# Attention normalization three slots later, its sum and the router's moments two, and a later, tighter S5 step sequence, in a hybrid layer kernel on one core

## What is computed

```python
x = x + s6(_layernorm(x), Wi, bi, Wx, bx, Wdt, bdt, A_log, Dp, Wo, bo, gamma, beta)   # "attention a"
x = x + moe(_layernorm(x), Wg, W1, W2, W3)
x = x + s5(_layernorm(x), Lambda_re, Lambda_im, B, C, D, log_step)                    # "attention b"
x = x + moe(_layernorm(x), Wg, W1, W2, W3)
...
# s6, for each batch: a selective scan with 256 channels and 64 states
h = exp(delta_t[..., None] * A) * h + (delta_t * x_t)[..., None] * B_t
y_t = C_t * sum(h, -1)
...
z = (y + xs * Dp) * silu(res) @ Wo + bo + residual
return gamma * (z - mean(z)) / sqrt(var(z) + 1e-5) + beta
...
# moe: 8 experts, the two best of each row, weights by softmax of their logits
y_e = (silu(x @ W1_e) * (x @ W2_e)) @ W3_e
```

## Time and profile before

| | |
|---|---|
| median of 3 runs | 1909.16 us (1908.35 to 1910.12) |
| the profiled execution | 1909.07 us, span 1907.2 us |
| busy DVE | 1523.3 us, 80% of the span |
| busy POOL | 1513.7 us, 79% |
| busy PE | 1360.6 us, 71% |
| busy ACT | 1293.1 us, 68% |
| the turns' lengths, turns 3 to 6 | 218.1, 218.4, 218.5, 218.4 us |
| mean granted TensorE clock | 0.846 of 2.4 GHz |
| HBM traffic | 63 GB/s over the span |

### The profile page before, as it was taken

The page is one execution under the profiler, slowest core; times in us unless marked ns, Lnnn a source line. Parts: engine busy times, 40 slices in busy tenths (PEclk is TensorE's granted clock), DMA queues, the critical chain, the costliest instruction groups (busy, mean ns, idle before and its releaser), DMA issues.

```text
span 1907.2 us, 19073 instructions
## 1 busy us (share of the span) xinstructions
PE 1360.6 (71%) x5928; PEld 605.4 (32%) x5928; DVE 1523.3 (80%) x2109; ACT 1293.1 (68%) x2285; POOL 1513.7 (79%) x888
## 2 busy tenths in 40 slices
PE   3236458677886887768876878767787788668958
PEld 1001123233332333324331343324332343224535
DVE  3989988887879888897989878898878978795222
ACT  4457668686877777677777777777777868655423
POOL 0899998978998799987998889986988789983212
PEclk8556569889987989889888889889898899869979
DMA  3511411122101311132101401131111211100000
GB/s 95 183 46 69 160 45 50 48 89 94 56 36 61 133 50 34 45 108 94 56 23 48 159 27 52 47 110 73 50 50 48 104 78 50 45 28 1 7 1 6
DMA packets 38749, 121.90 MB, mean 64 GB/s; under 512 B 5876, under 2 KB 21111, under 8 KB 26359
## 3 DMA queue, kind: packets, MB, share of 16 engines
q1 hardware_dynamic: 37062, 120.67, 17.7%
q10 hardware_dynamic: 1584, 0.01, 0.0%
HBM read 109.13 MB, written 11.53 MB: 63 GB/s over the span
## 4 chain that ended last, share of the span: by engine, by line
PE 27%; POOL 22%; ACT 16%; DVE 13%; issue 5%; DVEq 0%; POOLq 0%; ACTq 0%
POOL w L843 16%; DVE h L1145 8%; PE bankH L499 7%; PE bankY L512 6%; PE bankG L499 6%; ACT da L733 5%; POOL x L786 3%; ACT yk L694 3%; PE ys L566 3%; ACT L733 2%; PE bankG L469 1%; DVE aq L1083 1%; ACT L681 1%; ACT nrm L628 1%; PE bankY L493 1%
## 5 line engine op out<-in xcount | busy, mean ns | idle before, releaser
L1145 DVE TENSOR_TENSOR_SCAN h<-da,w 128x512 f32<-128x512 f32 x1024 | 1190.5, 1206 | 177.2 <-ACT da L733 138.0
L843 POOL TENSOR_TENSOR w<-ur,br 128x1024 f32<-128x1024 f32 x512 | 1193.6, 2364 | 33.0 <-DVE h L1145 20.8
L733 ACT ACTIVATE da<-dr,al 128x511 f32<-128x511 f32 x1024 | 683.1, 690 | 221.8 <-DVE h L1145 219.2
L566 PE MATMUL ys<-h,wsum 128*32 128x512 f32 x2048 | 329.7, 721 | 229.6 <-DVE h L1145 203.3
L499 PE MATMUL bankH<-nT,w 128*128 128x512 f32 x512 | 312.7, 695 | 95.8 <-DVE aq L1083 63.8
L786 POOL TENSOR_TENSOR x<-x,yk 128x512 f32<-128x512 f32 x128 | 163.1, 1274 | 258.3 <-ACT yk L694 228.9
L499 PE MATMUL bankG<-nT,w 128*128 128x512 f32 x512 | 293.0, 656 | 28.3 <-DVE aq L1083 28.3
L512 PEld LDWEIGHTS bankY<-w,aq 128*128 128x128 f32 x2048 | 260.0, 201 | 87.8 <-issue 78.2
L512 PE MATMUL bankY<-w,aq 128*128 128x128 f32 x2048 | 266.6, 286 | 11.1 <-DVE aq L1083 6.5
L694 ACT ACTIVATE yk<-bankY,rt 128x128 f32<-128x128 f32 x512 | 156.3, 366 | 131.4 <-PE bankY L512 111.9
L566 PEld LDWEIGHTS ys<-h,wsum 128*32 128x32 f32 x2048 | 43.2, 115 | 435.5 <-DVE h L1145 400.1
(11 more groups left out here) (178 smaller groups left out, 1069.2 us busy)
## 6 DMA issues: line engine op xcount, KB each, us to landing
br<-b_rows SPq DMA_DIRECT2D x64, 1024.0 KB, 5.0
dr<-d_rows SPq DMA_DIRECT2D x16, 1024.0 KB, 6.6
ur<-u_rows SPq DMA_DIRECT2D x16, 1024.0 KB, 7.2
d_rows<-vh SPq DMA_DIRECT2D x16, 256.0 KB
u_rows<-th SPq DMA_DIRECT2D x16, 256.0 KB
xnew<-in_L_attn_a_x_dram SPq DMA_DIRECT2D x8, 256.0 KB, 5.4
w<-in_L_ffn_W_dram SPq DMA_DIRECT2D x2, 1024.0 KB, 11.1
x<-in_L_attn_a_x_dram SPq DMA_DIRECT2D x8, 256.0 KB, 9.0
```

The costliest lines, as they stand in the source:

```text
L566: ins = nc.tensor.matmul(ys[32 * q:32 * q + 32, :], wsum[:, :], h[:, (DUOS * t.b + 2 * group + q // 2) % H_RING, q % 2, :], start=(n == 0) ...
L733: A(da[duo % D_RING][:, k % 2, 1:L], dr[:, half, q, 1:L], ACT.Exp, scale=nega[:, QUADS * half + q, n:n + 1]).then_inc(decay_ready, 1)
L843: G.tensor_tensor(w[:, turn_duo % W_RING, :, :], ur[:, half, q:q + 2, :], br[:, chunk % B_RING, row:row + 1, :].to_broadcast([128, 2, L]), ...
L1145: V.tensor_tensor_scan(h[:, turn_duo % H_RING, k % 2, :], da[duo % D_RING][:, k % 2, :], w[:, turn_duo % W_RING, k % 2, :], 0.0, ALU.mult, ...
```

## The change

Four numbers of the table change, and with them where steps stand.

- ACT's normalization 1 stands 9 slots behind its moments instead of 6 (slot 16 instead of 13).
- POOL's attention sum stands at slot 19 instead of 17.
- DVE's moments 2 stand at slot 18 instead of 16, and with them `rstd` 2 (24 instead of 22) and `normalize` 2 (26 instead of 24). The transpose x1T stays at slot 26.
- S5_AT is 79 instead of 77: moments 3, `rstd` 3, `normalize` 3, uT, P1, P2 and DVE's steps on them come two slots later. s5 comes at 93 (before 92) and s5t stays at 95.

```diff
-S5_AT = output_slot(1, E - 1) + SUM_LAG - 3
+S5_AT = output_slot(1, E - 1) + SUM_LAG - 1
...
-LN_AT = [PRE_AT - 6, 7, 16, S5_AT, MOE_AT[2] - 8]
-RSTD_LAG, NORM_LAG = 6, 6
+LN_AT = [PRE_AT - 6, 7, 18, S5_AT, MOE_AT[2] - 8]
+RSTD_LAG, NORM_LAG, GATED_NORM_LAG, ATTENTION_SUM_LAG = 6, 6, 9, 12
...
-    (S5_AT + 15, "post", "H", "s5"), (S5_AT + 18, "post", "Y", "s5t"),
+    (S5_AT + 14, "post", "H", "s5"), (S5_AT + 16, "post", "Y", "s5t"),
...
-                yield at + NORM_LAG + (2 if k == 2 else 0)
+                yield at + (GATED_NORM_LAG if k == 1 else NORM_LAG + 2 if k == 2 else NORM_LAG)
...
-                yield LN_AT[1] + NORM_LAG + 4
+                yield LN_AT[1] + ATTENTION_SUM_LAG
```

## The result

The changed kernel takes 1934.38 us (median of 4, 1932.77 to 1935.83), the kernel before 1909.57 beside it (1908.35 to 1910.12). The ratio is 1.0131, with a 95% interval of 1.0115 to 1.0147: slower by 24.8, or 1.3%. The forecast was 1926.7 in a range of 1907 to 1936, so sign and range held, and the sum of 17.6 was 7.2 short. The profiled execution is at the upper end, 1935.83, with a span of 1934.0 instead of 1907.2; the traces therefore differ by 26.8.

The account below looks back on a forecast made before the run. Four nearly equally busy engines, DVE most (1523.3 of 1907.2 us), were taken to hold each other up in turn. Terms 6.0 + 1.3 + 7.2 - 0.6 + 3.7 = 17.6 on 1909.1 gave 1926.7, range 1907 to 1936.

Parts of the forecast that it names:

- The waits of part 1: Attention normalization and router moments, turns 2 to 7: DVE's wait falls at slot 14, grows at slot 26; gain worth 0.
- the 49.2 that was set as a sign: Slot 26's scan, counted behind slot 0: if it started earlier than 49.2, the forecast would be wrong.
- Rival A: The waits saved before slot 14 and at slot 77 stay saved: 22.2 less 3.7 at the end, 1890.6; chance 0.13.
- The waits of part 2: S5, turns 1 to 6: no wait at the moments, 2.4 before L1106 at slot 88, 1.6 before slot 100.
- of the 2.2 about 1.5 is left: S5: stepsB starts 2.2 earlier, but the ys sum behind it falls into half clock and takes 0.7 longer.
- Part 1's 1.0 a turn: Router normalization between two yk pairs holds bank Y; x1T and slot 32's decay come 1.0 later, 6 x 1.0 = 6.0.
- No cover is left, so the whole 1.0 arrives: Slot 32: DVE already waits 0.47 for that decay, so the transpose's whole delay lengthens each of six turns.
- Turn 1: No late expert work there; attention product and rstd wait for later steps: 1.3 longer, between 0 and 3.5.
- Part 2's 1.2 a turn: S5: yT step L1122 comes 1.3 later, delaying dt1 and slot 100's decay; about 1.2 a turn, 6 x 1.2 = 7.2.
- Part 3's 3.7: Behind the last scan: later normalization of z delays sum, moments, last late output and transpose by 3.7, between 2 and 5.5.
- B: Rival: half-clock stretches swallow each turn's 2.2, only about 3.5 in all is left; 1912.5, chance 0.17.
- C: Rival: PE's longer waits make half-clock stretches grow, 1.7 more in five turns; 1935, chance 0.20.

Follow-up runs that it names:

- e4: Changed kernel with unread matmuls added, six ahead of the transpose x1T and one ahead of the router's matmuls; 1930.1 us.
- e3: Changed kernel with ACT's router normalization one slot later (slot 27), behind both yk pairs of the last late output; 1934.9 us.
- e11: Changed kernel with two repairs: router's normalization at slot 27, C1 and dt0 two slots later, behind P1 and P2; 1932.7 us.
- e5: Kernel before with unread matmuls added at five places (1 ahead of x1T, 1 router, 10 stepsB, 2 s5, 8 behind s5t); 1881.8 us, ratio 0.9865.
- e10: Kernel before with the S5 part of the change alone, and C1 and dt0 moved behind P1 and P2; 1913.9 us.
- e8: Changed kernel with unread matmuls added at five places (6 ahead of x1T, 1 router, 6 stepsB, 10 s5, 8 behind s5t); 1911.5 us.
- e9: Kernel before with the attention part of the change alone, and the router's normalization at slot 27, behind both yk pairs; 1915.4 us.
- e12: Kernel before with ten unread matmuls added at one place alone, ahead of stepsB; 1907.9 us, ratio 0.9992.
- e7: Kernel before with the S5 part alone, and unread matmuls at five places (1 ahead of x1T, 1 router, 6 stepsB, 10 s5, 8 behind s5t); 1909.1 us.
- e1: Kernel before with the attention part of the change alone, S5 left at slot 77; 1932.3 us, ratio 1.0126.

## Why the prediction was right, and by how much not

- **The waits of part 1, right.** Slot 14: 3.74 (3.7 forecast). Moments 2: 0.53 (0.6). Slot 26: 2.07 (2 or more), its scan at 49.14 behind slot 0, against 49.17 before: below the 49.2 that was set as a sign, but by no more than the kernel before itself. ACT's normalization waits for POOL's nm, and x1T is 0.95 later (1.0). Rival A, the saved waits staying saved, is out. The rule of the Trainium skill that was weighed there (Perfetto Trace Analysis, Optimization Strategy) is not borne out by the trace: two gaps of the busiest engine became shorter, 5.29 to 3.74 and 2.07 to none, and the turn 3.4 longer.
- **The waits of part 2, right in part by luck.** No wait at the S5 moments, 2.37 at L1106 (2.4), 1.96 at slot 100 (1.6). But the forecast's own terms don't give 2.4 at L1106: 1.39 stood there, DVE was to come 2.2 earlier against its scans and P2 0.2 later, and that makes 3.8. DVE came 1.3 later than that because of the two decay waits, 0.56 and 0.74, that the forecast lacks. The same 0.56 is why "of the 2.2 about 1.5 is left" holds: counted from slot 65, sres comes only 1.5 earlier, while stepsB and the sum behind it take no longer together than before (4.62 from the start of the one to the end of the other, 4.71 before), not 0.7 longer as the forecast had it.
- **Part 1's 1.0 a turn, mis-sized.** It was 2.5 at slot 32: 1.0 of order as forecast and 1.5 of half clock on the matmuls behind x1T, which the step priced at the duration they had before (and e4 shows that without any half clock there even the 1.0 is covered). "No cover is left, so the whole 1.0 arrives" was wrong the other way: slot 65's wait gave back 1.1. Six turns bring 6 x 1.34 = 8.0 instead of 6.0. Turn 1 brings 0.7 instead of 1.3, and not by the route forecast: slot 32's scan is 0.4 earlier there, and the loss stands at slot 65, whose wait grows from 1.77 to 2.97.
- **Part 2's 1.2 a turn, mis-sized.** L1122 came 1.36 later (1.3 forecast). The s5 matmuls and, in part, the sum ahead of dt1 ran at half clock, behind 6.20 of idle time on PE; the forecast had looked for such a stretch at C1 only. Turns 2 to 6 bring 5 x 2.08 = 10.4, turn 1 1.2; 11.6 instead of 7.2. Turn 7 gained 0.9 (0.6).
- **Part 3's 3.7, mis-sized.** Normalization and sum came 3.0 later at the moments (3.1). The last late output's matmuls then took 3.65 instead of 2.05, behind 3.46 of idle time, and those behind x1T lost 1.3 more: 6.6. With PE kept busy at the router alone, 3.0 of the 6.6 was gone (e4).
- The first turn is 0.9 longer. Its length is 160.9 to 163.0 in the fourteen kernels with no pattern to it, so I don't count that as the change's. The pieces make 8.0 + 0.7 + 11.6 - 0.9 + 6.6 + 0.9 = 26.9, of 26.8 between the traces.
- **The frame of the sum was wrong.** It added a price for each part. Rivals B (a lead is swallowed by half clock) and C (half-clock stretches grow) were kept apart as alternatives with 0.17 and 0.20, but e3 and e4 show both in one turn. The change is 7.2 dearer than forecast by C's mechanism. That a repair of a single step gives nothing while the other part stands fits B's, which e4's rows show at two places; for e11 it is argued and not shown. The Trainium skill, TensorE: Matmul & The Clock Gate, Part 1, puts the ramp at under 1% of a typical span. The trace does not agree: with PE kept busy at five places 1.35% went (e5).

What stays open: why e10's turns and e8's don't settle, what in e11 holds the turn at 221.87, and why the whole 3.4 arrives whichever part is late. That normalization 1's own move is harmless in the turns is argued from e9 and not from a run of its own.

## What to carry to other kernels

Price a delay on a busy engine's supplier twice: once for the order, once for what TensorE's longer idle time does to the clock of the matmuls behind it. Don't add up the prices of two parts of a change in a loop that repeats to 0.01 us; run each alone, and undo the suspected cause as well as the part. Where matmuls on the critical path run at half clock behind idle time, matmuls that nobody reads, placed in a bank already claimed, can be worth more than a reordering: here they brought 26, and every reordering that was tried cost time. They have to be tried in place, since the same ten helped in e5 and did nothing in e12.

## What the runs showed that was not expected

Full turns had one of three lengths in eleven of fourteen kernels: 215.04, 218.45 or 221.87, which are 3.41 and 3.42 apart, each to 0.03 us. They hold although the way there differs: of the kernels with 218.45, slot 80 stands at 141.27 behind slot 0 in the kernel before and at 138.90 in e7. No experiment here shows what sets them. The other three (e1, e8, e10) wander by 0.5 to 1.1.

Twenty-two matmuls a turn whose results are thrown away, some 13 us of PE's time in turn 4, made the kernel 26 us faster, and the mean granted clock rose from 0.846 to 0.879.
